# An attention stage on one Trainium2 core: its engine loops written out as straight-line code with constant waits

## The chip, the cores and the metric

The kernel runs on one core of a Trainium2 chip (trn2). The metric is the time of one execution on the device, in microseconds (us). The program is written engine by engine: TensorE (PE in the profile; PEld is its weight load), VectorE (DVE), ScalarE (ACT), GpSimd (POOL) and SyncE (SP, which issues the DMAs) each have their own instruction stream, and they meet only through semaphores. Each engine has a sequencer that reads its stream.

## The reference

A residual stream `x` of shape (4, 1024, 256) passes through six sublayers, each on a layer norm of `x`: a quantised linear layer, linear attention, the quantised layer again, a routed MLP, softmax attention, the routed MLP again. The changed stage is the softmax attention, with 16 heads of 128 and no mask:

```python
qkv = (x @ w_qkv).reshape(b, s, NUM_HEADS + 2 * NUM_KV, HEAD_DIM)
...
logits = jnp.einsum('bkpsd,bktd->bkpst', q, k) * scale
attn = jax.nn.softmax(logits.astype(jnp.float32), axis=-1)
combined = jnp.einsum('bkpst,bktd->bkpsd', attn, v.astype(jnp.float32)).astype(v.dtype)
...
return combined @ w_out
```

## The kernel before

All of `x` stays in the core's memory. `attention_phase` (from L1231) works on the four batches in two groups of two (`gi`, GB = 2). A **unit** is one head of one batch: 32 units a group (`UNITS`), 64 in all. Every product is made of three matmuls on a high and a low part (`split3`, L35 to L37).

A unit has eight **slots**, one for each 128 rows of queries. In slot `i` PE does, in this order (`unit` in the tensor block): the first half of the transposes of the probabilities of two slots ago (`turn(back, i, 0)`: four 128x128 transposes into the one buffer `at_ps_t`, L1552); the scores of this slot (6 matmuls, `at_ps_s`); three matmuls of values (`at_ps_o`); the second half of the transposes (`turn(back, i, 1)`); three more of values; and then the slot's **jobs** (table `JOBS`): projections K, VT, Q of the next unit (6 matmuls of 512 columns each), turning of V (4 transposes), or a piece Y of the output projection of the last unit (6 matmuls of 256 columns). Slots 2, 3 and 6 have a job Y alone; all others have more than that.

Since `at_ps_t` is one buffer, each half must be taken out before the next is turned: ACT rounds it to the high part (`probT_high`, L1353, counted by `s_ph`), DVE subtracts that for the low part (`probT_low`, L1409, counted by `s_pl`), and then PE may turn the next half. So PE waits before each first half for two things, written as two statements:

```python
pe.wait_ge(s_exp, TB * back + i + 1)
if slot >= 3 or has_last:
    pe.wait_ge(s_pl, 2 * TB * back + 2 * i)
turn(back, i, 0)
```

They are L1586 and L1588. Before the second half (L1596) it waits for `s_pl` alone. `s_exp` counts the exponentials, which are ready long before; `s_pl` is DVE's word that `at_ps_t` is free.

Each engine runs `Fori(0, 2)` over `gi` (PE L1601, DVE L1474, ACT L1396, POOL L1331), and inside it `sweep` (L1288) calls one unit FIRST, one MID, a loop `Fori(1, H - 1)` of 14 rounds of two MID units (L1293), one MID, one LAST and a TAIL. At the start of a group DVE takes the layer-norm statistics of `x` (`ln_statistics`, L341), POOL the inverse root, DVE normalises (L169), and PE turns the result (L1608) before the first scores.

The lists of the built program below name the waits in brackets on the next instruction shown; instructions that only wait have no row of their own.

Of the kernel before, what the change touches and what calls it, by code (L numbers as in the profile page):

```python
# [16 lines left out]
H, HD = 16, 128  # L17
# [1189 lines left out]
def taken_in(mode, slot, late):  # L1207

    return [(bank, kind, part) for bank, at, kind, part in jobs_of(mode)
            if slot is None or ((kind, part) in LATE) == late and slot == at + late]  # L1210
# [26 lines left out]
def attention_phase(nc, sh, w_in):  # L1237

    WK, WQ, WV, WO = 0, 1, 2, 3
    with ExitStack() as ctx:  # L1240
# [44 lines left out]
        def unit_of(kind, u):  # L1285
            return u - 1 if kind == "Y" else u + 1

        def sweep(eng, gi, unit):  # L1288

            u0 = gi * UNITS  # L1290
            unit(FIRST, u0, 0, gi)
            unit(MID, u0 + 1, 1, gi)
            with eng.Fori(1, H - 1) as h:  # L1293
                for b in range(GB):
                    unit(MID, u0 + h * GB + b, b, gi)
            unit(MID, u0 + UNITS - 2, 0, gi)
            unit(LAST, u0 + UNITS - 1, 1, gi)
            unit(TAIL, u0 + UNITS, 0, gi)

        @block.sync  # L1300
        def _(sp):
            def load(h, part, n):
                if n is not None:
                    sp.wait_ge(s_wl[part], n)
                sp.dma_start(wst[:, part, :], w_in[bass.ds(h, 1), :, part * D:(part + 1) * D]
                             .rearrange("a p d -> p (a d)")).then_inc(s_wdma[part], 16)

            for part in (WK, WV, WQ, WO):
                load(0, part, None)
            with sp.Fori(1, H) as h:  # L1310
                for part in (WK, WV, WQ, WO):
                    load(h, part, h)
            with sp.Fori(0, H) as h:
                for part in (WK, WV, WQ, WO):
                    load(h, part, h + H)

        @block.gpsimd
        def _(pool):
            def split(part, n, used, count):

                pool.wait_ge(s_wdma[part], 16 * n + 16)
                if count is not None:
                    pool.wait_ge(used, count)
                nc.gpsimd.tensor_tensor(wh[:, part, :], wst[:, part, :], zero[:], ALU.add).then_inc(s_wh[part], 1)  # L1324
                pool.wait_ge(s_wh[part], n + 1)
                nc.gpsimd.tensor_tensor(wl[:, part, :], wst[:, part, :], wh[:, part, :].bitcast(F32),
                                        ALU.subtract).then_inc(s_wl[part], 1)

            nc.gpsimd.memset(zero[:], 0.0).then_inc(s_zero, 1)
            pool.wait_ge(s_zero, 1)  # L1330
            with pool.Fori(0, 2) as gi:  # L1331
                ln_rstd(nc, pool, sh, ln, gi, GB * TB)
                n = gi * H

                split(WK, n, None, None)
                split(WV, n, None, None)
                split(WQ, n, None, None)
                split(WO, n, None, None)
                with pool.Fori(1, H) as h:  # L1340
                    m = gi * H + h
                    done = GB * m
                    split(WK, m, s_made["K"], parts["K"] * done)
                    split(WV, m, s_made["VT"], parts["VT"] * done)
                    split(WQ, m, s_made["Q"], parts["Q"] * done)
                    split(WO, m, s_made["Y"], parts["Y"] * done)

        @block.scalar
        def _(act):
            def probT_high(u, i, half):  # L1350

                act.wait_ge(s_pT, 2 * TB * u + 2 * i + half + 1)
                nc.scalar.activation(ph[:, i // TC, 4 * half:4 * half + 4, (i % TC) * P:(i % TC + 1) * P],  # L1353
                                     ps_t[:], ACT.Copy).then_inc(s_ph, 1)

            def job_high(mode, u, parity, slot, late=False):
                for bank, kind, part in taken_in(mode, slot, late):
                    if kind == "Y":
                        continue
                    v = unit_of(kind, u)  # L1360
                    vpar = 1 - parity
                    act.wait_ge(s_made[kind], parts[kind] * v + part + 1)
                    src = ps_job[bank][:]
                    if kind == "VT":
                        nc.scalar.activation(vT[:, part * CH:(part + 1) * CH], src, ACT.Copy).then_inc(s_taken[kind], 1)
                    elif kind == "K":
                        nc.scalar.activation(kh[:, vpar, part * CH:(part + 1) * CH], src, ACT.Copy).then_inc(s_high[kind], 1)
                    elif kind == "Q":
                        nc.scalar.activation(qh[:, part * CH:(part + 1) * CH], src, ACT.Copy, scale=SC).then_inc(s_high[kind], 1)
                    else:  # L1370
                        nc.scalar.activation(vh[:, vpar, TC * part:TC * part + TC, :].rearrange("p a b -> p (a b)"),
                                             src, ACT.Copy).then_inc(s_high[kind], 1)

            def out_high(u, half):
                act.wait_ge(s_o, 2 * u + half + 1)
                nc.scalar.activation(oh[:], ps_o[:], ACT.Copy).then_inc(s_oh, 1)

            def unit(mode, u, parity, gi):
                has_last, has_own = mode != FIRST, mode != TAIL
                for slot in range(TB):  # L1380
                    back, i = (u - 1, slot + TB - 2) if slot < 2 else (u, slot - 2)
                    turned = has_last if slot < 2 else has_own
                    if turned:
                        probT_high(back, i, 0)
                    job_high(mode, u, parity, slot, late=True)
                    if turned:
                        probT_high(back, i, 1)
                    if has_own:
                        act.wait_ge(s_max, TB * u + slot + 1)
                        nc.scalar.activation(prob[:, slot % 4, :], ps_s[slot % 2][:], ACT.Exp, bias=nmax[:, slot:slot + 1],  # L1390
                                             accum_out=rsum[:, parity, slot:slot + 1]).then_inc(s_exp, 1)
                    if slot in (1, 5) and has_last:
                        out_high(u - 1, slot // TC)
                    job_high(mode, u, parity, slot)

            with act.Fori(0, 2) as gi:  # L1396
                for c in range(NC * GB):
                    act.wait_ge(s_xT, NC * GB * gi + c + 1)
                    nc.scalar.activation(xh[:, c // NC, :, (c % NC) * CH:(c % NC + 1) * CH],
                                         ps_s[c % 2][:].rearrange("p (k t) -> p k t", k=KT), ACT.Copy).then_inc(s_xh, 1)  # L1400
                job_high(AHEAD, gi * UNITS - 1, 1, None)
                sweep(act, gi, unit)

        @block.vector
        def _(dve):
# [65 lines left out]
                        out_low(u - 1, slot // TC)  # L1471
                    job_low(mode, u, parity, slot, gi)

            with dve.Fori(0, 2) as gi:  # L1474
                tile0 = gi * GB * TB
                ln_statistics(nc, dve, sh, ln, gi, tile0, GB * TB)

                def normalise(c):
                    for j in range(TC):
                        last = layernorm_tile(nc, sh, prob[:, c, j * D:(j + 1) * D], x_tile(sh, tile0 + c * TC + j), c * TC + j)  # L1480
                    last.then_inc(s_xn, 1)

                def input_low(c):
                    dve.wait_ge(s_xh, NC * GB * gi + c + 1)
                    at = (slice(None), c // NC, slice(None), slice((c % NC) * CH, (c % NC + 1) * CH))
                    nc.vector.tensor_tensor(xl[at], ps_s[c % 2][:].rearrange("p (k t) -> p k t", k=KT),
                                            xh[at].bitcast(F32), ALU.subtract).then_inc(s_xl, 1)

                dve.wait_ge(ln.rstd, gi + 1)
                normalise(0)  # L1490
                normalise(1)
                for c in range(2, NC * GB):
                    input_low(c - 2)
                    normalise(c)
                input_low(NC * GB - 2)
                input_low(NC * GB - 1)
                job_low(AHEAD, gi * UNITS - 1, 1, None, gi)
                sweep(dve, gi, unit)

        @block.tensor  # L1500
        def _(pe):
# [96 lines left out]
                    values_part(slot, 1)  # L1598
                    job(mode, u, parity, slot)

            with pe.Fori(0, 2) as gi:  # L1601
                for c in range(NC * GB):
                    pe.wait_ge(s_xn, NC * GB * gi + c + 1)
                    if c >= 2:
# [68 lines left out]
```

## Time and profile before

| | us |
|---|---|
| median of three timed runs | 3950.33 |
| lowest, highest | 3947.76, 3950.85 |
| span of the profiled execution | 3947.1 |
| attention stage in it | about 995 to 3766 |
| PE busy in it | 3462.2 (88%) |

The time of an execution holds the span and some 3 us around it. "Idle before" in a row is the time for which the engine did nothing before that instruction, and the name behind "<-" is what ended it; "issue" means that the profile shows nothing it waited for. Instructions that only wait, compute registers or branch are not counted as busy and have no row. The start of unit n is taken as the start of its first matmul of scores: unit 1 starts at 1067.72 us, unit 2 at 1109.64, unit 16 at 1695.77, unit 30 at 2281.90, unit 31 at 2323.76, unit 33 at 2453.3.

### The profile page before, as it was taken

How to read it: one execution, taken by the hardware profiler on the slowest of the kernel's cores; microseconds unless marked ns; L12 is line 12 of the kernel's file. 1: busy time of each engine (PE TensorE's matmuls, PEld its weight loads, DVE VectorE, ACT ScalarE, POOL GpSimd, SP SyncE). 2: the span in 40 equal slices, each digit the busy share in tenths (PEclk: the TensorE clock that was granted, in tenths of full speed). 3: DMA queues.
4: the chain of work that ended last, by engine and by line, in shares of the span. 5: the costliest groups of instructions: out<-in, count | busy, mean ns of one | idle time of the engine just before them, and what ended most of it. 6: DMA issues, size and time to landing. Idle time of an engine off the chain costs nothing. (4 is left out here: it accounts for less than half of the span.)

```text
span 3947.1 us, 58123 instructions
## 1 busy us (share of the span) xinstructions
PE 3462.2 (88%) x19206; PEld 2904.9 (74%) x19206; DVE 2832.7 (72%) x5007; ACT 1989.1 (50%) x3566; POOL 754.9 (19%) x833
## 2 busy tenths in 40 slices
PE   2799898616799999999999997999999999999925
PEld 1687787515588888888888875888888888888725
DVE  7687787888666666766676665676676667667676
ACT  3555565522455555555555553555555555555512
POOL 4456565542100001000001001000010000010021
PEclk7899999857899999999999998999999999999967
DMA  1110000000000000000000000000000000000001
GB/s 47 47 36 15 31 24 27 8 24 1 15 6 5 5 5 11 5 5 5 5 5 11 5 2 11 6 5 5 5 8 8 5 5 5 5 11 1 1 25 43
DMA packets 40790, 49.76 MB, mean 13 GB/s; under 512 B 4224, under 2 KB 37888, under 8 KB 40064
## 3 DMA queue, kind: packets, MB, share of 16 engines
q1 hardware_dynamic: 40704, 48.68, 4.0%
q8 instruction: 45, 0.74, 0.1%
q14 instruction: 41, 0.34, 0.0%
HBM read 44.48 MB, written 4.19 MB: 12 GB/s over the span
## 5 line engine op out<-in xcount | busy, mean ns | idle before, releaser
L1353 ACT ACTIVATE at_probT_hi<-at_ps_t 128x512 fp32r<-128x512 f32 x1024 | 612.1, 598 | 1020.1 <-PE at_ps_t L1552 1019.9
L1409 DVE TENSOR_TENSOR at_probT_lo<-at_ps_t,at_probT_hi 128x512 fp32r<-128x512 f32 x1024 | 706.2, 690 | 406.0 <-ACT at_probT_hi L1353 395.4
L1552 PE MATMUL at_ps_t<-ident,at_prob 128*128 128x128 f32 x4096 | 625.8, 275 | 21.5 <-DVE at_probT_lo L1409 20.5
L1460 DVE TENSOR_REDUCE at_neg_max<-at_ps_s 128x1 f32<-128x1024 f32 x512 | 624.6, 1220 | 14.4 <-PE at_ps_s L37 1.8
L1552 PEld LDWEIGHTS at_ps_t<-ident,at_prob 128*128 128x128 f32 x4096 | 488.4, 140 | 161.5 <-DVE at_probT_lo L1409 70.8
L1390 ACT ACTIVATE at_prob<-at_ps_s,at_neg_max 128x1024 f32<-128x1024 f32 x512 | 569.6, 1112 | 8.1 <-DVE at_neg_max L1460 8.1
L1324 POOL TENSOR_TENSOR at_w_hi<-at_w_raw,at_zero 128x256 fp32r<-128x256 f32 x128 | 94.5, 738 | 2441.6 <-PE at_ps_job L37 2441.6
L35 PE MATMUL at_ps_o<-at_probT_hi,at_v_lo 128*128 128x512 f32 x1024 | 446.8, 436 | 2.8 <-DVE at_oT_lo L1443 2.8
L35 PE MATMUL at_ps_s<-at_k_hi,at_q_lo 128*128 128x512 f32 x1024 | 447.1, 437 | 0.0
L37 PE MATMUL at_ps_o<-at_probT_lo,at_v_hi 128*128 128x512 f32 x1024 | 404.4, 395 | 0.0
L37 PE MATMUL at_ps_s<-at_k_lo,at_q_hi 128*128 128x512 f32 x1024 | 403.8, 394 | 0.0
L36 PE MATMUL at_ps_o<-at_probT_hi,at_v_hi 128*128 128x512 f32 x1024 | 400.5, 391 | 0.0
L36 PE MATMUL at_ps_s<-at_k_hi,at_q_hi 128*128 128x512 f32 x1024 | 399.3, 390 | 0.0
L35 PE MATMUL at_ps_job<-at_xnT_hi,at_w_lo 128*128 128x512 f32 x768 | 305.4, 398 | 2.0 <-DVE at_q_lo L1433 1.9
L37 PE MATMUL at_ps_job<-at_xnT_lo,at_w_hi 128*128 128x512 f32 x768 | 303.1, 395 | 0.0
L36 PE MATMUL at_ps_job<-at_xnT_hi,at_w_hi 128*128 128x512 f32 x768 | 300.3, 391 | 0.0
L1423 DVE SCALAR_TENSOR_TENSOR x_resident<-at_ps_job,at_row_inv,x_resident 128x256 f32 x512 | 224.0, 480 | 31.5 <-PE at_ps_job L37 9.7
L37 PEld LDWEIGHTS at_ps_s<-at_k_lo,at_q_hi 128*128 128x128 f32 x1024 | 192.3, 188 | 45.5
L37 PEld LDWEIGHTS at_ps_o<-at_probT_lo,at_v_hi 128*128 128x128 f32 x1024 | 192.2, 188 | 45.1
L686 DVE SCALAR_TENSOR_TENSOR x_resident<-li_ps_y,li_rnorm,x_resident 128x256 f32<-128x256 f32 (+1 forms) x512 | 212.4, 478 | 6.5
L36 PEld LDWEIGHTS at_ps_s<-at_k_hi,at_q_hi 128*128 128x128 f32 x1024 | 195.0, 190 | 23.8
L35 PEld LDWEIGHTS at_ps_o<-at_probT_hi,at_v_lo 128*128 128x128 f32 x1024 | 193.7, 189 | 23.4 <-DVE at_oT_lo L1443 3.7
(301 smaller groups left out, 6736.7 us busy)
## 6 DMA issues: line engine op xcount, KB each, us to landing
at_w_raw<-attn_w SPq DMA_DIRECT2D x128, 128.0 KB, 2.3
li_wq_raw<-lin_q_w SPq DMA_DIRECT2D x64, 128.5 KB, 2.1
x_resident<-x SPq DMA_DIRECT2D x4, 1024.0 KB, 10.5
li_wo_raw<-lin_out_w SPq DMA_DIRECT2D x8, 512.0 KB, 3.3
li_xn<-lin_out_w SPq DMA_DIRECT2D x8, 512.0 KB, 4.2
out<-x_resident SPq DMA_DIRECT2D x4, 1024.0 KB, 8.5
fa_w_raw<-mlp_w SPq DMA_DIRECT2D x2, 1024.0 KB, 5.0
fb_w_raw<-mlp_w SPq DMA_DIRECT2D x2, 1024.0 KB, 4.7
```

What stands on the lines that cost most here:

```text
L35: nc.tensor.matmul(out, al, bh, start=start, stop=False)
L36: nc.tensor.matmul(out, ah, bh, start=False, stop=False)
L37: return nc.tensor.matmul(out, ah, bl, start=False, stop=stop)
L686: nc.vector.scalar_tensor_tensor(xt, ps_y[:, j, 0:D], rnorm[:, j:j + 1], xt, ALU.mult, ALU.add).then_inc(s_x, 1)
L1324: nc.gpsimd.tensor_tensor(wh[:, part, :], wst[:, part, :], zero[:], ALU.add).then_inc(s_wh[part], 1)
L1353: nc.scalar.activation(ph[:, i // TC, 4 * half:4 * half + 4, (i % TC) * P:(i % TC + 1) * P], ps_t[:], ACT.Copy).then_inc(s_ph, 1)
L1390: nc.scalar.activation(prob[:, slot % 4, :], ps_s[slot % 2][:], ACT.Exp, bias=nmax[:, slot:slot + 1], accum_out=rsum[:, parity, slot:slot ...
L1409: nc.vector.tensor_tensor(pl[at], ps_t[:], ph[at].bitcast(F32), ALU.subtract).then_inc(s_pl, 1)
L1423: last = nc.vector.scalar_tensor_tensor(xt, src[:, j * D:(j + 1) * D], rinv[:, vpar, tile:tile + 1], xt, ALU.mult, ALU.add)
L1460: nc.vector.tensor_reduce(nmax[:, slot:slot + 1], ps_s[slot % 2][:], AX.X, ALU.max, negate=True).then_inc(s_max, 1)
L1552: last = nc.tensor.transpose(ps_t[:, j, :], prob[:, i % 4, kt * P:(kt + 1) * P], sh.ident[:])
```

## The change

The loops of the attention stage become Python loops that run when the program is built, on all five engines; the rounds stand one behind the other, and each count that is waited for is a constant. The order of the work, the buffers and the counts are the same.

```diff
-            with eng.Fori(1, H - 1) as h:
+            for h in range(1, H - 1):
                 for b in range(GB):
                     unit(MID, u0 + h * GB + b, b, gi)
...
-            with sp.Fori(1, H) as h:
+            for h in range(1, H):
                 for part in (WK, WV, WQ, WO):
                     load(h, part, h)
-            with sp.Fori(0, H) as h:
+            for h in range(0, H):
...
-            with pool.Fori(0, 2) as gi:
+            for gi in range(0, 2):
...
-                with pool.Fori(1, H) as h:
+                for h in range(1, H):
...
-            with act.Fori(0, 2) as gi:
+            for gi in range(0, 2):
...
-            with dve.Fori(0, 2) as gi:
+            for gi in range(0, 2):
...
-            with pe.Fori(0, 2) as gi:
+            for gi in range(0, 2):
```

In the built program PE's stream grows from 4237 to 18355 entries, DVE's from 2085 to 4402, ACT's from 1018 to 2818.

**PE, around the first half of transposes behind a job Y.** Before, in the inner loop (the last rows of the job, then `turn(back, i, 0)`, then the scores):

```order
2079 L35 MATMUL at_ps_job<-at_w_hi,at_oT_lo 128x256
2080 L36 MATMUL at_ps_job<-at_w_hi,at_oT_hi 128x256
2081 L37 MATMUL at_ps_job<-at_w_lo,at_oT_hi 128x256
2082 L1586 REGISTER_ALU
2083 L1588 REGISTER_ALU [waits at_exp]
2084 L1552 MATMUL at_ps_t<-ident,at_prob 128x128 [waits at_pl]
2085 L1552 MATMUL at_ps_t<-ident,at_prob 128x128 x3
```

The same place in the changed program:

```order
2002 L35 MATMUL at_ps_job<-at_w_hi,at_oT_lo 128x256
2003 L36 MATMUL at_ps_job<-at_w_hi,at_oT_hi 128x256
2004 L37 MATMUL at_ps_job<-at_w_lo,at_oT_hi 128x256
2005 L1552 MATMUL at_ps_t<-ident,at_prob 128x128 [waits at_pl,at_exp]
2006 L1552 MATMUL at_ps_t<-ident,at_prob 128x128 x3
```

The two register instructions are gone. Before, one of them carried the wait for `at_exp` and the transpose itself the wait for `at_pl`. Now the transpose carries the wait that was written first, `at_exp`, and the one that was written second, `at_pl`, stands in an instruction that only waits, ahead of it (in the list, the first name in the brackets). That is so at 510 of the 512 first halves; the other two, in the FIRST units, wait for `at_exp` alone. Before each second half `at_pl` is carried by the transpose both before and after.

**DVE, from one group to the next.** Before, the rows at the end of the outer loop's body:

```order
1287 L1419 REGISTER_ALU
1288 L1423 SCALAR_TENSOR_TENSOR x_resident<-at_ps_job,at_row_inv,x_resident 128x256 [waits at_made_Y]
1289 L1423 SCALAR_TENSOR_TENSOR x_resident<-at_ps_job,at_row_inv,x_resident 128x256
1290 L1474 REGISTER_ALU
1291 L1474 COMPARE_AND_BRANCH
```

and at its head, to which that branch goes back:

```order
787 L1474 UNCONDITIONAL_BRANCH
788 L1474 ISA
789 L341 BN_STATS ln_stats<-x_resident 128x6
790 L341 ISA
791 L341 BN_STATS ln_stats<-x_resident 128x6
```

Now the statistics of the second group (`L341 BN_STATS`, 16 of them) stand right behind the last L1423 of the first, with no branch and no register instructions.

**PE, in the routed MLP ahead of the stage** (`scatter`, unchanged by the edit): a place that has the two forms of wait side by side. In the list the reused semaphores go by older names: `li_wql` is `s_x` (DVE's word that the buffer is free), `li_wq1` is `s_ol`.

```order
1495 L1182 MATMUL fa_ps_r<-fa_oo_lo,fa_hotT 128x256 [waits li_wql,li_wq1]
1496 L1183 MATMUL fa_ps_r<-fa_oo_hi,fa_hotT 128x256
1497 L1182 MATMUL fa_ps_r<-fa_oo_lo,fa_hotT 128x256
1498 L1183 MATMUL fa_ps_r<-fa_oo_hi,fa_hotT 128x256
1499 L1182 MATMUL fa_ps_r<-fa_oo_lo,fa_hotT 128x256 [waits li_wql]
```

Row 1495 has `s_x` in an instruction ahead of the matmul, row 1499 in the matmul itself. Nothing of it moves.

## Rows read from the trace of the kernel before

**Rows 1.** The page: its head and the busy time of each engine.

```profile
span 3947.1 us, 58123 instructions
PE 3462.2 (88%) x19206; PEld 2904.9 (74%) x19206; DVE 2832.7 (72%) x5007; ACT 1989.1 (50%) x3566; POOL 754.9 (19%) x833
```

**Rows 2.** Windows, units 1, 16, 30: length; busy PE, PEld, DVE, ACT, POOL; clock.

```profile
1067.72:1109.64 41.92, 41.91 (x232) 34.96 (x230) 29.14 (x42) 23.31 (x43) 1.43 (x2) 1.00 0.01 4
1695.77:1737.63 41.86, 41.84 (x231) 34.94 (x230) 29.15 (x42) 23.31 (x43) 1.41 (x2) 1.00 0.00 0
2281.90:2323.76 41.86, 41.84 (x231) 34.94 (x230) 29.13 (x42) 23.29 (x43) 1.41 (x2) 1.00 0.00 1
```

**Rows 3.** Timeline, unit 16, slots 1 to 3: start, length, engine, line.

```profile
1705.60 0.69 DVE L1409 TENSOR_TENSOR at_probT_lo<-at_ps_t,at_probT_hi 128x512 fp32r<-128x512 f32 x1 [0.53 <-ACT at_probT_hi L1353]
...
1706.63 0.59 PEld L1552 LDWEIGHTS at_ps_t<-ident,at_prob 128*128 128x128 f32 x4
...
1709.38 0.60 PE L1552 MATMUL at_ps_t<-ident,at_prob 128*128 128x128 f32 x4
1710.02 0.60 ACT L1353 ACTIVATE at_probT_hi<-at_ps_t 128x512 fp32r<-128x512 f32 x1 [1.88 <-PE at_ps_t L1552]
...
1710.65 0.69 DVE L1409 TENSOR_TENSOR at_probT_lo<-at_ps_t,at_probT_hi 128x512 fp32r<-128x512 f32 x1 [0.45 <-ACT at_probT_hi L1353]
...
1711.12 0.28 PE L37 MATMUL at_ps_job<-at_w_lo,at_oT_hi 128*128 128x256 f32 x1
1711.39 0.42 PEld L1552 LDWEIGHTS at_ps_t<-ident,at_prob 128*128 128x128 f32 x4 [0.20 <-DVE at_probT_lo L1409]
```

**Rows 4.** Waits (total, times, longest): whole span; units 1-30; unit 0; 32; 31 with TAIL.

```profile
PEld at_ps_t L1552 <- DVE at_probT_lo L1409: 70.8, 215, 1.7
...
PEld at_ps_t L1552 <- DVE at_probT_lo L1409: 18.8, 90, 0.2
...
PEld at_ps_t L1552 <- DVE at_probT_lo L1409: 7.5, 6, 1.7
...
PEld at_ps_t L1552 <- DVE at_probT_lo L1409: 7.9, 7, 1.7
...
PEld at_ps_t L1552 <- DVE at_probT_lo L1409: 8.9, 11, 1.2
```

**Rows 5.** Timeline, `scatter`: row 1495 of the list, then row 1499's form of wait.

```profile
988.81 0.48 DVE L1050 SCALAR_TENSOR_TENSOR x_resident<-fa_ps_r,fa_weight,x_resident 128x256 f32<-128x256 f32 x1
...
989.40 0.18 PEld L1182 LDWEIGHTS fa_ps_r<-fa_oo_lo,fa_hotT 128*128 128x128 f32 x1 [0.57 <-issue]
...
989.59 0.48 DVE L1050 SCALAR_TENSOR_TENSOR x_resident<-fa_ps_r,fa_weight,x_resident 128x256 f32<-128x256 f32 x1
...
990.12 0.19 PEld L1182 LDWEIGHTS fa_ps_r<-fa_oo_lo,fa_hotT 128*128 128x128 f32 x1 [0.19 <-DVE x_resident L1050]
```

**Rows 6.** Timeline, router: PE behind DVE through an instruction that only waits (L1106).

```profile
850.17 0.23 DVE L952 TENSOR_SCALAR fa_logit<-fa_logit,fa_br 128x8 f32<-128x8 f32 x1
...
850.52 0.29 PEld L1111 LDWEIGHTS fa_ps_r<-ident,fa_logit 128*128 128x128 f32 x2 [22.63 <-issue]
```

**Rows 7.** Timeline of DVE between the groups; then, from the waits, PE's start there.

```profile
2378.75 1.66 DVE L1423 SCALAR_TENSOR_TENSOR x_resident<-at_ps_job,at_row_inv,x_resident 128x256 f32 x4 [1.14 <-PE at_ps_job L37]
2382.54 0.75 DVE L341 BATCH_NORM_STATS2 ln_stats<-x_resident 128x6 f32 x2 [2.13 <-issue]
...
PE at_ps_s L1608 <- DVE at_prob L169: 36.7, 8, 15.7
```

**Rows 8.** DMA queues (packets, MB): 1400 to 2200 us; 1068 to 1152 us; whole span.

```profile
q1 hardware_dynamic: 5760, 5.25, 2.1%
...
q8 instruction: 3, 0.05, 0.2%
q14 instruction: 2, 0.02, 0.1%
...
q8 instruction: 45, 0.74, 0.1%
```

## The prediction

> **What bounds the kernel now.** I read the page's head first, then the attention stage unit by unit, then one unit's timeline, then who waited for whom. PE is busy for 88% of the span [rows 1]. A MID unit takes 41.86 us, whether it stands in the inner loop (unit 16) or is written out beside it (unit 30), and PE is busy for 41.84 of it at the full clock of 2.4 GHz [rows 2]. The reader is to see two things there: the stage, 64 such units, is PE's, and a back edge of the inner loop shows nowhere in a unit's length. What PE still loses is in the timeline of slots 2 and 3 [rows 3]: the second half of transposes ends at 1709.98 (1709.38 + 0.60), ACT takes it from 1710.02 to 1710.62, DVE from 1710.65 to 1711.34, and PE loads the next half's weights at 1711.39. Meanwhile PE has three matmuls of values and a job Y, whose last matmul starts at 1711.12; then it is idle, 0.20 us before the weight load. The waits say how often: 90 times in units 1 to 30, 18.8 us in all, which is three a unit at 0.21 us, the three slots with a job Y alone [rows 4]. So the path of the stage is PE's matmuls, plus, three times a unit, one handoff from DVE to PE.
>
> **The change, part by part.** *The waits on PE.* This is the term that I expect to decide. At 510 first halves the wait for `at_pl`, which DVE's low part ends, moves from the transpose into an instruction ahead of it that only waits; the early `at_exp` takes its place on the transpose. Where `at_pl` comes last, its handoff changes form. The trace has both forms side by side [rows 5]. Carried by the matmul: DVE ends at 990.07 (989.59 + 0.48), the weight load starts at 990.12, 0.05 us later, and in attention it is the same 0.05 (1711.34 to 1711.39) [rows 3]. Through an instruction ahead: DVE ends at 989.29 (988.81 + 0.48), the load starts at 989.40, 0.11 us later; the router's handoff in that form is 0.12 (850.40 to 850.52) [rows 6]. So the new form costs 0.06 to 0.07 us; I take 0.06, from the pair that differs in nothing else. It can't lie beside other work, since PE is idle at these places.
>
> How many: 215 waits in the whole stage [rows 4]. 2 x 90 are in MID units, with 90 again in units 33 to 62, all at first halves. The other 35 are 6 and 7 in the two FIRST units and 11 in each end (LAST with TAIL). By the order of the program 3 + 4 of the first and 2 + 2 of the ends stand at second halves, whose wait keeps its form. That leaves 180 + 24 = 204 handoffs, all on PE's path. 204 x 0.06 = 12.2 us more.
>
> At the other first halves the new instruction is covered. The least work that PE has there between the last half turned and the next is three matmuls of values and one K part, in slot 1; there DVE ends at 1706.29 (1705.60 + 0.69) and the weights are loaded at 1706.63 [rows 3], 0.34 us later, where the new form needs 0.11. If DVE were later there by 0.23 us, these would pay too. What is queued behind the new instruction on PE is all that follows in the slot, scores first; in a slot with a job Y nothing of it could run anyway, since the transposes come first in PE's order. ACT and DVE only get more time before the next half.
>
> *The waits elsewhere.* The other waits on PE that go ahead of a matmul (for V, the output's low part, the weights) and DVE's 64 for `at_made_Y` at slot 2 are for things long done, or are followed by slack: behind that job DVE waits 0.4 us for ACT at the next half, as at the one shown [rows 3]. I cost them at nothing. ACT, POOL and SP wait as before and none of them is on the path.
>
> *The register and branch instructions.* They lie beside PE's matmuls: unit 30, with no back edge in or behind it, is as long as unit 16 [rows 2]. Both hold the register instructions, so the rows bound their cost only through the handoffs, which are already 0.03 (ACT, DVE) and 0.05 (PE) [rows 3], the same as where waits are constants [rows 5]. I take 0.
>
> *The back edge of the outer loop.* DVE's last piece of the first group ends at 2380.41 (2378.75 + 1.66); the statistics of the second start at 2382.54, after 2.13 us of "issue" [rows 7]. This is on the path: PE is out of work and waits for DVE's normalised input (36.7 us over both groups). Written out, the statistics follow at once. That takes 2.1 us off, once. What is late next is DVE's own chain of statistics, which only moves up. The smaller start-up before the first group I put at 0 to 0.2 us and at 0.1 in the sum.
>
> *Instructions to fetch.* In 800 us of the inner loop no instructions are fetched, only weights; where the code is written out, PE's queue (q8, by its share) brings 3 packets of 16 KB (45 make 0.74 MB) in two units [rows 8]. Written out, all 64 units stream like that. Unit 1, written out, is 0.06 us longer than unit 16; unit 30, also written out, isn't [rows 2]. So the price is 0 to 0.06 a unit, 0 to 3.4 us over the 56 units that leave the inner loop; I take 0, since unit 30 is the nearer case: it has the loop's steady state before it, and unit 1 the filling of the pipeline.
>
> The Trainium skill has a rule that would speak for more: its page "Runtime: NRT & Kernel Launch", section "Instruction fetch mechanics", says that a taken branch whose target is no longer in the fetched window stalls for the fetch, and that this is a reason to unroll. By that rule for every back edge, DVE's 26 in the inner loops would give back 26 x 2.1 = 55 us. The rows show such a stall at the outer back edge alone and no fetch within the inner loop, so the sum has it once.
>
> *The sum.* 3947.1 + 12.2 - 2.1 - 0.1 = 3957.1 for the profiled execution; the median before lies 3.2 above its span (3950.3), so 3960.3, 0.25% more than before.
>
> **The rivals.** *The instruction that waits costs nothing here* (same time). It would need PE's queue to be full behind it, so that the wait is read early. For: at most first halves it is. Against: where it matters PE is idle, and the idle handoffs of this form all show 0.11 to 0.12 [rows 5, 6]. Then only the edge remains: 3950.3 - 2.2 = 3948.1.
>
> *Constant waits are noticed sooner* (faster). If the compare with a register were part of the 0.05 us, up to 204 x 0.05 = 10.2 us could go, with the edge 12.4: 3937.9. Against: the handoff with constants in `scatter` has the same 0.05 [rows 5]. The case of a stall at each inner back edge, 3895, belongs here too and has the rows against it.
>
> *Fetching falls behind* (slower by more). PE's stream turns from a loop that stays into one that comes by DMA throughout. At three packets in two units a packet has some 28 us to come, so it decides only if a stream is not asked for ahead. If each of the 96 packets of 64 units cost PE what the one miss cost DVE, 2.1 us, that is 200 us: 4160. For: the miss exists [rows 7]. Against: units 1 and 30 stream and lose at most 0.06 [rows 2, 8]. A milder form, 0.06 a unit, gives 3963.7 and lies in my range.
>
> **How the numbers follow.** The wait in its new form, 0.70, with its own range 3957 to 3966 (0.05 to 0.07 at 190 to 204 places, 0 to 3.4 for fetching); the wait for nothing, 0.15; sooner or edges, 0.05; fetching behind, 0.10. A measurement of this kernel can tell about 0.2%, 7.9 us, from no change, so slower begins at 3958.2, and a fifth of the likeliest case falls below it. Slower: 0.70 x 0.8 + 0.10 = 0.66; same: 0.14 + 0.15 = 0.29; faster 0.05. The range takes in the second case at its low end and the milder fetching at its high: 3947.5 to 3967.
>
> **What would show it.** A MID unit of 42.05 us (41.86 + 3 x 0.06), units 1 to 30 together 5.4 us longer; PE's weight load 0.11 us behind DVE's end where it was 0.05, and the idle time before it 0.26 instead of 0.20, now perhaps put down to "issue"; the 2.13 us before the statistics gone; q8 at some 140 packets with no gap on PE at regular distance. Wrong would be: MID units of 41.9 (the wait is free), or less (the registers did cost); units of uneven length (fetching); or a gap at a second half, which would mean that ACT or DVE became later.

## The result, and the profile after

| | before | after |
|---|---|---|
| median of 12 runs, us | 3948.88 | 3959.66 |
| lowest, highest, us | 3944.68, 3950.85 | 3957.34, 3963.71 |
| span of the profiled execution, us | 3947.1 | 3962.0 |

After over before is 1.0030, with a 95% interval of 1.0022 to 1.0039: slower by 10.8 us of 3949. The forecast was 3960.3. (The before column pools the three runs shown ahead with nine more.)

The page of the changed kernel, its head and DMA queues, answers to [rows 1] and [rows 8]:

```profile
span 3962.0 us, 52040 instructions
PE 3455.0 (87%) x19206; PEld 2902.2 (73%) x19206; DVE 2835.7 (72%) x5007; ACT 1987.8 (50%) x3565; POOL 755.9 (19%) x833
...
q8 instruction: 139, 2.28, 0.2%
```

6083 instructions are gone (58123 before), all of them register, branch and wait instructions and their like, since matmuls and DVE's work have the same counts; PE's instruction queue (q8) brings 139 packets where it brought 45. That q8 is PE's is shown further down by E3 and E4: it brings 45 packets with PE's loops and 139 without them, whatever the other engines do. Fewer instructions did not make the kernel faster.

The windows of units 1, 16 and 30, columns as in [rows 2]:

```profile
1072.36:1114.45 42.09, 41.81 (x231) 34.94 (x230) 29.12 (x42) 23.31 (x43) 1.44 (x2) 1.00 0.02 4
1703.40:1745.46 42.06, 41.76 (x231) 34.93 (x230) 29.13 (x42) 23.30 (x43) 1.35 (x2) 1.00 0.00 1
2292.33:2334.39 42.06, 41.78 (x231) 34.93 (x230) 29.12 (x42) 23.30 (x43) 1.35 (x2) 1.00 0.00 1
```

A MID unit is 0.20 us longer than before (42.06 against 41.86), at the same clock (1.00) and with as much work. PE's busy time even fell by 0.08: the new time is idle time. The timeline of unit 16, at the end of slot 2, shows where (start, length, engine, line, and in brackets the idle time before):

```profile
1718.27 0.69 DVE L1409 TENSOR_TENSOR at_probT_lo<-at_ps_t,at_probT_hi 128x512 fp32r<-128x512 f32 x1 [0.45 <-ACT at_probT_hi L1353]
...
1718.74 0.28 PE L37 MATMUL at_ps_job<-at_w_lo,at_oT_hi 128*128 128x256 f32 x1
1719.08 0.42 PEld L1552 LDWEIGHTS at_ps_t<-ident,at_prob 128*128 128x128 f32 x4 [0.27 <-issue]
1719.11 0.63 PE L1552 MATMUL at_ps_t<-ident,at_prob 128*128 128x128 f32 x4
```

DVE ends at 1718.96 (1718.27 + 0.69) and the weights are loaded at 1719.08: 0.12 us later, where [rows 3] had 0.05. The idle time is 0.27 instead of 0.20, and it is now put down to "issue", since the late semaphore is waited for by an instruction that has no row. Over the 90 such places of units 1 to 30 the step from DVE's end to the weights is 0.115 us, and was 0.053. So the same handoff has changed its name in the waits as well. They are (total, times, longest) those of the whole stage, of units 1 to 30, and of unit 31 with TAIL:

```profile
PEld at_ps_t L1552 <- issue: 72.7, 204, 1.8
...
PEld at_ps_t L1552 <- issue: 24.5, 90, 0.3
...
PEld at_ps_t L1552 <- issue: 7.1, 9, 1.2
PEld at_ps_t L1552 <- DVE at_probT_lo L1409: 2.3, 2, 1.2
```

In units 1 to 30 the 90 waits cost 24.5 us instead of 18.8 [rows 4], 0.063 each. 204 of the stage's 215 handoffs changed form. The 11 that stand at second halves kept theirs, two of them in each end, as the last row shows.

DVE between the groups, which answers to [rows 7]:

```profile
2389.90 1.66 DVE L1423 SCALAR_TENSOR_TENSOR x_resident<-at_ps_job,at_row_inv,x_resident 128x256 f32<-128x256 f32 x4 [1.14 <-PE at_ps_job L37]
2391.48 4.64 DVE L341 BATCH_NORM_STATS2 ln_stats<-x_resident 128x6 f32<-128x256 f32 x14
```

The 2.13 us of "issue" are gone; the statistics start before the last piece has ended. From the start of unit 31 to that of unit 32 it was 94.18 us and is 92.03. These 2.15 us are a net of three things. The statistics come 2.21 us earlier behind the last piece (2.13, and 0.08 of overlap). The nine handoffs of the LAST unit and TAIL cost 0.5 more. And behind the statistics 0.46 us come from PE's granted clock. These are the windows from the job list's first matmul to unit 32, before and after; the granted clock stands behind the five busy times (0.89 and 0.93 of full speed):

```profile
2405.42:2417.95 12.53, 11.48 (x47) 8.39 (x45) 4.59 (x6) 5.10 (x8) 0.00 (x0) 0.89 0.00 0
2414.34:2426.43 12.09, 11.02 (x47) 8.07 (x45) 4.59 (x6) 5.10 (x8) 0.00 (x0) 0.93 0.00 0
```

PE's clock is at 1.2 GHz in both traces when that list starts; it is back at 2.4 GHz 2.7 us later in before and 1.7 us later in the changed kernel.

The stage, from its first statistics to the first instruction of the MLP behind it, took 2771.01 us and takes 2781.66, 10.65 more; the medians differ by 10.8. The two profiled spans differ by 14.9: 4.4 of it lie ahead of the stage, in code that is the same in both (the stage begins at 995.30 and at 999.75), and the profiled execution of the changed kernel is its slowest of the 12. Such shifts come in all the traces: in the experiments below the stage begins anywhere from 989.9 to 995.8, and the code behind it takes anywhere from 176.9 to 181.1 us (180.7 in before, 180.6 in the changed kernel), the same code each time. They are as large as what the change does, so the length of a unit, which repeats to 0.05 us within a trace (units 2 to 30), carries the argument below, and the medians go beside it.

### The profile page after: what moved, and what is told of

Its sections match the earlier page's. It is cut to its first block and busy times, and to the rows that moved or that the text cites. A ratio compares the mean times of both kernels' runs of the same rounds, so it can differ in the third digit from the quotient of the medians.

```text
span 3962.0 us, 52040 instructions
## 1 busy us (share of the span) xinstructions
PE 3455.0 (87%) x19206; PEld 2902.2 (73%) x19206; DVE 2835.7 (72%) x5007; ACT 1987.8 (50%) x3565; POOL 755.9 (19%) x833
## 5 line engine op out<-in xcount | busy, mean ns | idle before, releaser
L1552 PE MATMUL at_ps_t<-ident,at_prob 128*128 128x128 f32 x4096 | 620.1, 274 | 40.3 <-DVE at_probT_lo L1409 22.0
L1552 PEld LDWEIGHTS at_ps_t<-ident,at_prob 128*128 128x128 f32 x4096 | 488.6, 140 | 174.7 <-issue 72.7
L1423 DVE SCALAR_TENSOR_TENSOR x_resident<-at_ps_job,at_row_inv,x_resident 128x256 f32<-128x256 f32 x512 | 223.9, 479 | 36.0 <-PE at_ps_job L37 19.5
```

Source lines behind the costliest of these rows:

```text
L1423: last = nc.vector.scalar_tensor_tensor(xt, src[:, j * D:(j + 1) * D], rinv[:, vpar, tile:tile + 1], xt, ALU.mult, ALU.add)
L1552: last = nc.tensor.transpose(ps_t[:, j, :], prob[:, i % 4, kt * P:(kt + 1) * P], sh.ident[:])
```

## The experiments

| kernel | median, us | over before, 95% interval | MID unit, us |
|---|---|---|---|
| before | 3948.88 | | 41.87 |
| after | 3959.66 | 1.0030 [1.0022, 1.0039] | 42.07 |
| E1: written out, waits swapped | 3944.21 | 0.9986 [0.9977, 0.9995] | 41.90 |
| E2: loops, waits swapped | 3962.19 | 1.0029 [1.0017, 1.0041] | 42.09 |
| E3: all written out but PE | 3946.36 | 0.9991 [0.9982, 1.0000] | 41.88 |
| E4: PE alone written out | 3960.64 | 1.0027 [1.0017, 1.0036] | 42.07 |
| E5: written out, jobs spread | 3926.01 | 0.9944 [0.9930, 0.9957] | 41.32 |
| E6: E5 with waits swapped | 3923.18 | 0.9937 [0.9923, 0.9950] | 41.32 |
| E7: after, second halves too | 3961.64 | 1.0034 [1.0021, 1.0048] | 42.08 |
| E8: loops, jobs spread | 3926.62 | 0.9944 [0.9931, 0.9958] | 41.32 |
| E9: E6 with V1 ahead of Y2 | 3912.78 | 0.9913 [0.9900, 0.9927] | 41.33 |
| E10: after with a third wait | 3959.51 | 1.0028 [1.0017, 1.0038] | 42.07 |

The MID unit is the mean of units 1 to 30. Each group was compared with runs of before on its own chip: 3951.01 for E1 to E4, 3948.24 for E5 to E8, 3949.03 for E9 and E10. The ratios count, not the differences between groups. In the rows of E3 and E4 the attention code stands ten lines further down: L1433 there is L1423 of the others, L1562 is L1552.

### Is it the form of the wait? E1 and E2

The change gave PE two things at once: straight-line code, and an instruction ahead of the transpose that carries the late wait. E1 keeps the first and undoes the second, by writing the late wait first, so that the transpose carries it:

```diff
-                        pe.wait_ge(s_exp, TB * back + i + 1)
                         if slot >= 3 or has_last:
                             pe.wait_ge(s_pl, 2 * TB * back + 2 * i)
+                        pe.wait_ge(s_exp, TB * back + i + 1)
                         turn(back, i, 0)
```

> The changed kernel with the two statements ahead of each first half of transposes in the other order, so that the late wait (at_pl) is carried by the transpose and the early one (at_exp) by the instruction ahead. Theory (the form of the late wait makes the loss): MID units back to 41.86 us, handoff 0.05 us, the edge's 2.1 us still saved, so about 2 us under the kernel before, near 3946.7, ratio to before 0.9995. Rival (straight-line code or fetching costs PE by itself): it stays with the changed kernel, MID units 42.07, some 3959.

E2 makes the same edit in the kernel before, with its loops: there the register instruction of `at_exp` then carries the wait for `at_pl`.

> The kernel before, loops kept, with only those two statements in the other order: now the register instruction carries the late wait. Theory: the loss comes without any straight-line code; a register instruction takes about as long from wait to next instruction as one that only waits, so 204 x 0.06 = 12 us over before (0.04 to 0.09 each gives 8 to 18), no 2.1 us saved: about 3961. Rival (straight-line code is the cause): no change, 3949.

Measured: E1 3944.21, E2 3962.19. E1 has as many instructions as the changed kernel (52040), E2 as many as before (58123): what is waited for changes places, and nothing is added. The windows of unit 16, first of E1 and then of E2:

```profile
1691.78:1733.68 41.90, 41.87 (x232) 34.94 (x230) 29.14 (x42) 23.32 (x43) 1.36 (x2) 1.00 0.00 1
```

```profile
1694.92:1737.04 42.12, 41.88 (x232) 34.96 (x230) 29.16 (x42) 23.32 (x43) 1.43 (x2) 1.00 0.00 0
```

And the handoff behind a job Y in the timeline, again E1 and then E2:

```profile
1706.66 0.69 DVE L1409 TENSOR_TENSOR at_probT_lo<-at_ps_t,at_probT_hi 128x512 fp32r<-128x512 f32 x1 [0.45 <-ACT at_probT_hi L1353]
...
1707.40 0.42 PEld L1552 LDWEIGHTS at_ps_t<-ident,at_prob 128*128 128x128 f32 x4 [0.21 <-DVE at_probT_lo L1409]
```

```profile
1709.80 0.69 DVE L1409 TENSOR_TENSOR at_probT_lo<-at_ps_t,at_probT_hi 128x512 fp32r<-128x512 f32 x1 [0.45 <-ACT at_probT_hi L1353]
...
1710.62 0.42 PEld L1552 LDWEIGHTS at_ps_t<-ident,at_prob 128*128 128x128 f32 x4 [0.28 <-issue]
```

With the late wait in the transpose, 0.05 us from DVE's end (1707.35) to the weights; with it in an instruction ahead, 0.13 (1710.49 to 1710.62), though that one is a register instruction of a loop. So the loss follows the form of the wait and not the loop: the swap takes 0.17 us a unit from the written-out kernel (42.07 to 41.90) and gives 0.22 to the looped one (41.87 to 42.09). The order of two statements is worth as much as the whole change.

E1's median is 6.8 us below before, and its stage doesn't show that: it is 1.5 us longer than the one of before (2772.47 against 2771.01), with 1.8 lost over 60 units of 41.90, 1.2 in unit 32, where the granted clock was 0.95 in that execution, and 1.8 won at the edge. The median can't be explained by the stage, then. In the two profiled executions E1 is 4.6 us shorter ahead of the stage and 3.7 behind it, in code that is the same in both. Why was not found, and no more than the 0.17 us a unit is claimed for the swap.

### Which engine's loop? E3 and E4

E3 writes out every engine but PE, E4 PE alone. The loops of `sweep` are chosen by engine, and the outer loops of the engines concerned likewise:

```diff
+        def looped(eng):
+            return eng is nc.tensor
...
+            if looped(eng):
+                with eng.Fori(1, H - 1) as h:
+                    rounds(h)
+            else:
+                for h in range(1, H - 1):
+                    rounds(h)
```

> DVE, ACT, POOL and SP written out as in the change, PE with its loops as before. Theory: PE's waits have their old form, MID units 41.86; DVE's edge is gone (2.1 us), and PE's own miss at the outer back edge is hidden behind DVE's statistics: about 2 us under before, 3946.8. Rival (DVE or ACT written out give the loss, or PE's back edge is next on the path): 3949 to 3961.

> PE alone written out, the other engines with their loops as before. Theory: all of the loss and nothing of the gain: MID units 42.07, DVE's 2.13 us before the statistics still there: 3949 + 12.4 = about 3961.5. Rival (the loss comes from the other engines): about 3949.

Measured: E3 3946.36, E4 3960.64. Unit 16 of E3, then of E4:

```profile
1696.06:1737.92 41.86, 41.84 (x231) 34.94 (x230) 29.13 (x42) 23.30 (x43) 1.35 (x2) 1.00 0.00 0
```

```profile
1694.72:1736.79 42.07, 41.77 (x232) 34.94 (x230) 29.16 (x42) 23.34 (x43) 1.43 (x2) 1.00 0.00 1
```

The loss is PE's alone, and the gain at the edge is not. In E4 (first row block), where DVE still loops, DVE's statistics of the second group come after a gap that E3 (second) hasn't:

```profile
2381.26 1.66 DVE L1433 SCALAR_TENSOR_TENSOR x_resident<-at_ps_job,at_row_inv,x_resident 128x256 f32 x4 [1.13 <-PE at_ps_job L37]
2385.37 5.00 DVE L341 BATCH_NORM_STATS2 ln_stats<-x_resident 128x6 f32 x15 [2.45 <-issue]
```

```profile
2379.14 1.66 DVE L1433 SCALAR_TENSOR_TENSOR x_resident<-at_ps_job,at_row_inv,x_resident 128x256 f32<-128x256 f32 x4 [1.14 <-PE at_ps_job L37]
2380.71 4.66 DVE L341 BATCH_NORM_STATS2 ln_stats<-x_resident 128x6 f32<-128x256 f32 x14
```

So the two terms of the sum come apart: writing out PE gives +0.2 us a unit, writing out DVE's outer loop takes some 2.2 off, once. From unit 31 to unit 32 E3 takes 91.36 and E4 95.08, where before takes 94.18 and the changed kernel 92.03. (0.6 of E3's 2.8 are the clock again: from the job list's first matmul to unit 32 it takes 11.94 us, and before 12.53.)

The gap has a mark in the DMA queues. In E4 DVE's last piece ends at 2382.92 and the statistics start at 2385.37; of instructions, this window holds one packet of 8 KB in the queue of the engines other than PE:

```profile
q14 instruction: 1, 0.01, 0.8%
```

All four traces in which DVE loops have one such packet there, and the statistics start 1.97 to 2.06 us behind its start. What differs is how soon it starts behind the last piece: 0.15 us in before (gap 2.13), 0.16 in E2 (2.15), 0.32 in E8 (2.38), 0.48 in E4 (2.45). In the changed kernel no packet comes there, and there is no gap. That fits a fetch of the code at the loop's head; q14 doesn't say for which engine a packet is, so it stays a reading.

### Is the price paid where PE has work? E7

E7 writes the early wait ahead of the second half's wait too, so that there also an instruction ahead carries `at_pl`:

```diff
                     if turned:
+                        pe.wait_ge(s_exp, TB * back + i + 1)
                         pe.wait_ge(s_pl, 2 * TB * back + 2 * i + 1)
                         turn(back, i, 1)
```

> The changed kernel with a second wait, for the exponentials that are long there, written ahead of the second half's wait for DVE's low part too, so that at second halves also an instruction ahead of the transpose carries the late wait. In a MID unit no second half is exposed: the next transposes' weights are loaded 0.08 us (slot 2), 0.1 (slot 5), 0.15 (slot 0) and 0.25 to 0.3 us (the others) behind DVE's end in the kernel before. My theory: only places at which PE is idle pay; at most slot 2 and 5 pay a little (0.11 needed against 0.08 and 0.11), so a unit of 42.07 to 42.11; the 11 stalled second halves in the FIRST, LAST and TAIL units pay 0.07 each, 0.8 us: 3960 to 3963. The rival, each such instruction costs 0.06 on PE wherever it stands, gives 8 x 0.06 = 0.48 more a unit, 42.55, and about 3990.

Measured: 3961.64, 0.0004 more in its ratio than the changed kernel, which is within the noise (the two intervals overlap). Its page counts 52552 instructions, 512 more than after: they were added. Unit 16:

```profile
1697.28:1739.36 42.08, 41.79 (x231) 34.94 (x230) 29.14 (x42) 23.32 (x43) 1.35 (x2) 1.00 0.00 1
```

Eight more such instructions in a unit cost 0.01 us together (the means are 42.078 and 42.068). The timeline of slot 2 shows one of them at the place with the least slack:

```profile
1709.90 0.68 DVE L1409 TENSOR_TENSOR at_probT_lo<-at_ps_t,at_probT_hi 128x512 fp32r<-128x512 f32 x1
...
1710.66 0.39 PE L37 MATMUL at_ps_o<-at_probT_lo,at_v_hi 128*128 128x512 f32 x1
1710.69 0.55 PEld L1552 LDWEIGHTS at_ps_t<-ident,at_prob 128*128 128x128 f32 x4
```

DVE ends at 1710.58 and the weights are loaded at 1710.69, 0.11 later. PE meanwhile runs the last matmul of values, and no idle time is shown. In the edges of the groups, where second halves do stall, all are now "issue" (unit 31 with TAIL: 11 times, where after has 9 and 2):

```profile
PEld at_ps_t L1552 <- issue: 9.6, 11, 1.2
```

The rival, 0.06 for each such instruction wherever it stands, would have given 42.55.

### Does the number of waits matter? E10

E10 puts a third wait, for something long done, between the two of the first half:

```diff
                         pe.wait_ge(s_exp, TB * back + i + 1)
                         if slot >= 3 or has_last:
+                            pe.wait_ge(s_max, TB * back + i + 1)
                             pe.wait_ge(s_pl, 2 * TB * back + 2 * i)
```

> The changed kernel with a third wait statement ahead of each first half, between the two: for DVE's row maximum of the same slot, which is even longer done than the exponential. The transpose carries the wait for the exponential, as in the change; the waits for the maximum and for DVE's low part stand ahead of it. It measures whether the price goes by the number of instructions that stand between the late wait and the transpose. If each costs PE the same 0.067 us at an exposed handoff, the step from the last matmul of Y to the first transpose grows again and a MID unit is 42.07 + 0.20 = 42.27, the whole 3970 to 3974. If the further wait shares an instruction with the late one, or is read for nothing, the unit stays at 42.07 and the whole at 3958 to 3962.

Measured: 3959.51, and at the handoff the picture of the changed kernel, 1709.78 to 1709.90:

```profile
1709.09 0.69 DVE L1409 TENSOR_TENSOR at_probT_lo<-at_ps_t,at_probT_hi 128x512 fp32r<-128x512 f32 x1 [0.45 <-ACT at_probT_hi L1353]
...
1709.90 0.42 PEld L1552 LDWEIGHTS at_ps_t<-ident,at_prob 128*128 128x128 f32 x4 [0.27 <-issue]
```

Its page counts 52040 instructions, as many as after: in the built program the instruction ahead of the transpose holds both waits, the third with the second, and the third costs nothing. Whether two instructions ahead would cost twice stays open; this run has only one.

### Without an exposed handoff: E5, E6 and E8

If the price is paid only where PE has run out of work, it must vanish when no slot is short of work. The three slots with a job Y alone get company, and no job's length changes:

```diff
-JOBS = [(0, "K", 0), (0, "VT", 0), (1, "K", 1), (2, "Y", 0), (3, "Y", 1), (4, "VT", 1),
-        (4, "V", 0), (5, "Q", 0), (5, "V", 1), (6, "Y", 2), (7, "Y", 3), (7, "Q", 1)]
+JOBS = [(0, "K", 0), (1, "VT", 0), (2, "Y", 0), (2, "Y", 1), (3, "K", 1), (4, "VT", 1),
+        (4, "V", 0), (5, "Q", 0), (6, "Y", 2), (6, "V", 1), (7, "Y", 3), (7, "Q", 1)]
```

E5 has this in the changed kernel, E6 in E1 (waits swapped), E8 in the kernel before (loops).

> The changed kernel with its waits as they are, but with the table of jobs in another order: VT of the first batch goes from slot 0 to slot 1, Y1 from slot 3 to slot 2, K1 from slot 1 to slot 3, V1 from slot 5 to slot 6, so that no slot has a job Y of one piece alone and every slot's last job takes PE at least 1.1 us. My theory: the exposed handoff, and with it the place where the form of the wait is paid, exists only where PE runs out of work before DVE's low part ends. Here it does not, so the three stalls of a MID unit (0.21 us each before, some 0.28 with the new form) go: a unit of 42.07 - 0.85 = 41.2 us, about 50 us less than the changed kernel, 3908 to 3914. If instead the new form costs its 0.07 at every first half, covered or not, the unit is 41.2 + 8 x 0.07 = 41.8. If moving the jobs makes others late (a job's input from DVE or ACT not ready), the unit stays at 41.9 to 42.1 with stalls at other lines.

> The same order of jobs, and the two wait statements of the first half swapped, so that the transpose itself carries the wait for DVE's low part. My theory: with no exposed handoff the form of the wait costs nothing, so the unit and the time are those of the kernel with spread jobs and unswapped waits, within 0.02 us a unit; about 3908 to 3912. The rival, a price at every first half, makes this one 0.5 us a unit, some 30 us, faster than the unswapped.

> The kernel before, with its loops, and the same order of jobs. My theory: where no handoff is exposed, writing the loops out changes nothing within a unit; this kernel has the unit length of the one with spread jobs written out, within 0.02 us, and is only about 2 us longer, by DVE's gap at the edge from one group to the next: 3910 to 3914. If the straight-line code costs something by itself that the stalls have so far hidden (fetching), this one is the faster.

Measured: 3926.01, 3923.18 and 3926.62. Unit 16 of E5, E6 and E8:

```profile
1685.79:1727.11 41.32, 41.32 (x231) 34.89 (x230) 28.79 (x42) 23.10 (x43) 1.35 (x2) 1.00 0.00 1
```

```profile
1691.51:1732.83 41.32, 41.32 (x232) 34.91 (x230) 28.78 (x42) 23.09 (x43) 1.36 (x2) 1.00 0.00 1
```

```profile
1691.28:1732.60 41.32, 41.32 (x231) 34.90 (x230) 28.81 (x42) 23.09 (x43) 1.42 (x2) 1.00 0.00 0
```

The three are equal to the hundredth: PE is busy for the whole unit, and the waits of units 1 to 30 list nothing for the transposes. So neither the form of the wait, nor the loops, nor the fetching costs anything where no handoff is exposed. The unit was forecast at 41.2. By the starts of its matmuls a stall did give back what it should: the step from Y's last matmul to the first transpose is 0.376 us in the changed kernel (mean of units 1 to 30) and 0.120 where it is covered, the next step 0.138 and 0.108, so 0.29 for each, 0.86 for three. The unit fell by 0.75. The other 0.11 is spread over its other matmuls, which follow each other a little more slowly when PE never pauses (16 steps to the last matmul of a scores group took 3.68 us together instead of 3.64).

The times were a miss, all three: 3908 to 3914, 3908 to 3912 and 3910 to 3914 were expected. In E5 the 60 units gave 45 us, 7 less than forecast, and the ends lost 15 us, on which the forecast had nothing. From the stage's first statistics to unit 0 E5 takes 38.47 us instead of 35.87, from unit 31 to unit 32 98.60 instead of 92.03, in units 0 and 32 2.8 more together, and from unit 63 to the stage's end 60.57 instead of 57.46. E5, E6 and E8 differ there among themselves too (98.60, 97.33 and 99.57 from unit 31 to 32), where handoffs are still exposed and the granted clock falls to 1.2 GHz for some us; that is why their times differ while their units don't.

### The lost part, and the best kernel: E9

Jobs take turns at two PSUM buffers by their place in the table. (A number behind a job is the third entry of its row: the batch for K, V and Q, the piece for Y.) Ahead of a group and in FIRST there are no jobs Y, and with V1 behind Y2 the jobs Q0, V1 and Q1 then follow each other in the same buffer. E9 is E6 with those two changed over:

```diff
-        (4, "V", 0), (5, "Q", 0), (6, "Y", 2), (6, "V", 1), (7, "Y", 3), (7, "Q", 1)]
+        (4, "V", 0), (5, "Q", 0), (6, "V", 1), (6, "Y", 2), (7, "Y", 3), (7, "Q", 1)]
```

> The written-out kernel with spread jobs and swapped waits, but with V1 ahead of Y2 in slot 6. The jobs take turns at two PSUM buffers by their place in the table; with V1 behind Y2, the three jobs Q0, V1 and Q1 stand in the same buffer one behind the other where there is no Y, that is in the job list ahead of a group and in the FIRST unit. V1 ahead of Y2 gives the turns of the kernel before there. In the runs with spread jobs so far a MID unit is 41.32 us (60 x 0.58 us less than the 41.90 of the written-out kernel with swapped waits), but the stage's start and the edge between the groups are longer than there: 38.5 against 36 us of start-up, 97.3 against 92.3 us from unit 31 to 32. My theory: the buffers' turns are the cause of most of that, so this one has units of 41.32 still, start-up of 36 and an edge of 92 to 94, some 8 us less than its forerunner: 3911 to 3917. The rival, that a LAST unit and TAIL without their spread jobs are longer by themselves (the Y jobs stand closer there), leaves the edge at 97: 3918 to 3923.

Measured: 3912.78. The windows from unit 31 to unit 32 and PE's waits for the job list in it, E6:

```profile
2311.30:2408.63 97.33, 68.56 (x336) 53.34 (x334) 56.77 (x99) 31.27 (x52) 9.02 (x11) 0.84 0.02 7
...
PEld at_ps_job L1524 <- DVE at_q_lo L1433: 1.8, 1, 1.8
PEld at_ps_job L35 <- DVE at_v_lo L1437: 1.6, 1, 1.6
PEld at_ps_job L35 <- DVE x_resident L1423: 1.2, 1, 1.2
```

and E9:

```profile
2306.54:2399.39 92.85, 66.85 (x336) 52.62 (x335) 56.59 (x99) 31.20 (x52) 9.02 (x11) 0.87 0.03 8
...
PEld at_ps_job L35 <- DVE at_q_lo L1433: 1.2, 1, 1.2
```

V waiting for Q's buffer, then Q for V's, 3.4 us together, are gone, as is the wait of a job Y for the buffer of the last one (1.2); a wait of 1.2 for Q's buffer takes their place, as in E1. That is 3.4 of the 4.5 us between the two windows; the rest was not taken apart, and the granted clock differs as well (0.84 and 0.87). Units of 41.33, a start-up of 35.84: E9 is 36 us below before (0.9913), and is the fastest kernel here. Its stage is 33 us shorter than that of before, and 32 of these are the stalls closed in 60 units (41.87 to 41.33); the other 3 us of the median are not in the stage.

## Why the prediction was right, point by point

**The bound.** It was PE's matmuls plus three handoffs a unit, and both halves hold: with the handoffs covered, the unit is PE's busy time and nothing else (41.32 of 41.32).

**The price of the new form.** I took 0.06 us from the pair in `scatter` [rows 5]. Per place it came out at 0.067: a MID unit grew by 0.20 where the sum had 0.18. At the starts of the matmuls two steps changed: from Y's last matmul to the first transpose 0.284 to 0.376 us, and from there to the second transpose 0.165 to 0.138. Over 60 units that is 11.9 us instead of 10.8.

**The count.** 204 was right, and the waits say it in one row (72.7, 204). The 24 outside the MID units cost about 1.4 us, by the waits of units 0 and 32 and the two ends taken before and after: 0.06 each, as in the sum.

**The covered first halves.** No stall appeared at any but the three slots; that a covered one costs nothing is shown by E5 against E6, and at second halves by E7.

**The other waits, the register and branch instructions.** 0 was right: E3 has them all removed on four engines, with a unit of 41.88, and E8 has them all with a unit of 41.32 as E5 and E6.

**The outer edge.** The term meant DVE's gap, and that was right: the statistics come 2.2 us sooner. That the stretch from unit 31 to 32 is shorter by 2.15, nearly the same number, is a coincidence: the sum had the handoffs of that stretch (0.5) in another term, and had no term for the granted clock behind the statistics (0.46 the other way). The gap itself is 2.13 to 2.45 us in the four traces with DVE's loop, so 2.1 was one draw of it. The 0.1 at the start-up was not there: 35.81 and 35.87.

**Fetching.** 0 was right, though PE's code now comes in 139 packets. Units 2 to 30 of the changed kernel take 42.05 to 42.08 us each, with no odd one among them, and E8, whose inner loops fetch nothing, is as fast within a unit as E5. The rule of the Trainium skill that I set against the rows ("Runtime: NRT & Kernel Launch", "Instruction fetch mechanics": a taken branch to a target that is no longer in the fetched window stalls) fits the one place where the rows showed such a stall, with its packet, and no other. The inner loops' back edges cost nothing, which also fits that rule if their bodies were still in the window, and no run shows the window; the mistake would have been to apply the rule to each back edge.

**The sum.** 10.0 us was forecast (12.2 - 2.1 - 0.1) and the stage grew by 10.65: 13.3 at the handoffs (11.9 in the MID units, 1.4 elsewhere), 2.2 off for DVE's gap and 0.5 off by the clock, with a rest of 0.1. So the handoffs cost 1.1 more than the sum had, and half of that was taken back by a term it didn't have. That the median came within 0.6 of the 3960.3 is in part luck: the median of before fell by 1.5 when nine runs were added. The step from span to median was luck as well: in every run of which both are on record an execution takes 1.7 to 2.1 us more than its span and not some 3, so of the 3.2 us between the span and the median of before more than 1 is that the profiled execution was one of the faster.

**A reading that was off.** The handoff to ACT is 0.04 us by the row shown (1709.98 to 1710.02), not 0.03; nothing hangs on it.

**The rivals.** The wait that costs nothing would have left 41.86 a unit; constants noticed sooner would show in E1, whose handoff has the same 0.05 as with registers; fetching that falls behind would show in E5 against E8. None of them happened.

## What to carry to other kernels

Where an engine waits for two things before an instruction, find out which comes last and whether the engine is idle by then: if so, the late wait belongs in the instruction itself and the one that is long satisfied in the instruction ahead. Here the order of two lines was worth 0.17 to 0.22 us in each of 60 units, 10 to 14 us of 3950, and loops against straight-line code nothing but some 2 us at one edge. Better still is to take the idle place away: spreading the same jobs so that every slot covers its handoff brought the fastest kernel, 36 us below before, and within a unit it made the form of the wait and the loops worth nothing.

## What the runs showed of the hardware that was not expected

- An early wait in the transpose and the late one ahead of it cost 0.067 us of a handoff where an instruction that only waits stands ahead (after: a third of the 0.20 a unit), and 0.075 where a register instruction of a loop does (E2: a third of 0.225). From DVE's end to the weights it is 0.115 and 0.125 us, against 0.053. So the kind of instruction makes little difference. With the early wait in it (E1), the same instruction ahead costs at most 0.01.
- In the changed kernel the second transpose follows the first 0.03 us sooner behind the longer handoff (0.138 us, before 0.165), so that a part of the loss comes back at once. In E2 it hardly does (0.162). Where the half is covered that step is 0.108.
- Such an instruction on PE costs nothing as soon as PE has work in progress: 8 more in a unit made it 0.01 us longer (E7), even at a place with 0.11 us between DVE's end and the load.
- A third wait joined the second in one instruction and was free (E10).
- DVE lost 2.13 to 2.45 us at the outer back edge in four traces. Some 2.0 of it lie behind the start of a packet of instructions and are nearly the same each time; the rest is how soon that packet starts.
